# Two-stage delta-block kernel: row block substitution for the 128-row inverses, a float32 Gram row, and scratch-to-scratch copies of diagonal blocks

## What is computed

```python
k = k / jnp.linalg.norm(k, axis=-1, keepdims=True)
K = jnp.tril(jnp.einsum('ntc,nsc->nts', k, k), k=-1)
A = K + jnp.eye(T, dtype=x.dtype)
u = jax.scipy.linalg.solve_triangular(A, v, lower=True)
score = jnp.einsum('nsk,ntk->nst', q, k)
y = jnp.einsum('nst,ntv->nsv', score, lr * u)
return y @ out_w + out_b
```

```python
h = jax.nn.silu(gate) * up
return jnp.einsum('bsh,dh->bsd', h, wd)
```

## Time and profile before

| | before |
|---|---|
| median of 3 runs | 1599.51 us |
| the profiled execution's own time | 1598.77 us |
| span of its instructions | 1597.0 us |
| granted TensorE clock, share of full speed | 0.999 |
| TensorE matmul busy | 1576.0 us (99%) |
| TensorE weight load busy | 1409.5 us (88%) |
| DVE / ACT / POOL busy | 1140.3 / 778.4 / 780.5 us |
| keys stage, main stage | to about 266 us; from 268 us |

### The profile page before, as it was taken

How to read it: one execution, slowest core, us unless ns; L and a number is a source line. 1 busy time by engine, 2 the same in 40 slices (tenths; PEclk the granted TensorE clock), 3 DMA queues, 4 the chain that set the end, 5 groups by cost and what they waited for, 6 DMA issues and landing times.

```text
span 1597.0 us, 29857 instructions
## 1 busy us (share of the span) xinstructions
PE 1576.0 (99%) x10758; PEld 1409.5 (88%) x10758; DVE 1140.3 (71%) x2813; ACT 778.4 (49%) x1504; POOL 780.5 (49%) x918
## 2 busy tenths in 40 slices
PE   8999999899999999999999999999999999999998
PEld 8999998788888888888888888888888888888887
DVE  6767774577777677777776777877776666666664
ACT  5766664344444444444444444444444444444443
POOL 5446872344444554444445544444444444444442
PEclk9999999999999999999999999999999999999999
DMA  7989998112222322222222222222222222222200
GB/s 238 338 301 302 322 312 271 60 61 73 74 74 73 113 74 73 73 74 74 73 74 96 90 73 73 73 69 69 70 94 75 74 73 73 74 70 71 67 24 27
DMA packets 150164, 178.19 MB, mean 112 GB/s; under 512 B 78850, under 2 KB 132098, under 8 KB 141826
## 3 DMA queue, kind: packets, MB, share of 16 engines
q1 hardware_dynamic: 150018, 176.28, 33.4%
HBM read 98.64 MB, written 77.59 MB: 110 GB/s over the span
## 4 chain that ended last, share of the span: by engine, by line
PE 80%; DVE 2%; ACT 1%; POOL 0%; issue 0%; DVEq 0%; POOLq 0%; ACTq 0%
PE ps L174 33%; PE ps L1088 22%; PE ps L1098 11%; PE ps L1008 5%; PE ps L1019 4%; PE ps L1002 4%; PE ps L1129 0%; DVE z_lo L1452 0%; PE ps L246 0%; DVE low L198 0%; DVE low L218 0%; POOL work L1624 0%; DVE bs L1592 0%; ACT h_hi L1287 0%; DVE late L1477 0%
## 5 line engine op out<-in xcount | busy, mean ns | idle before, releaser
L1664 POOL TENSOR_TENSOR hl<-late,hh 128x512 fp32r<-128x512 f32 x128 | 165.3, 1291 | 207.2 <-ACT hh L1270 207.2
L1098 PE MATMUL ps<-wdT,hh 128*128 128x256 f32 x744 | 198.3, 303 | 0.0
L1265 ACT ACTIVATE late<-ps 128x512 f32<-128x512 f32 x192 | 114.3, 595 | 169.7 <-PE ps L1088 169.7
L1447 DVE TENSOR_TENSOR late<-ps,late 128x512 f32<-128x512 f32 x192 | 132.7, 691 | 87.5 <-PE ps L1088 85.9
L1274 ACT ACTIVATE z_hi<-ps 128x256 fp32r<-128x256 f32 x128 | 48.9, 382 | 288.4 <-PE ps L1019 288.4
L1098 PE MATMUL ps<-wdT,hl 128*128 128x256 f32 x744 | 181.8, 281 | 0.3 <-DVE hl L1452 0.3
L1270 ACT ACTIVATE hh<-late 128x512 fp32r<-128x512 f32 x192 | 120.8, 629 | 109.7 <-DVE late L1447 109.7
L1610 POOL TENSOR_TENSOR sc<-ls,mhalf 128x4 f32<-128x4 f32 x64 | 65.1, 1016 | 192.9 <-DVE ls L1414 192.9
L1646 POOL TENSOR_TENSOR xhm_lo<-xh,xhm_hi 128x1024 fp32r<-128x1024 f32 x32 | 76.4, 2386 | 163.3 <-DVE xhm_hi L1523 163.3
L1088 PE MATMUL ps<-xh3T_hi,wgT 128*128 128x512 f32 x384 | 153.4, 400 | 1.1 <-DVE xh3T_lo L1452 1.1
L1088 PE MATMUL ps<-xh3T_lo,wuT 128*128 128x512 f32 x384 | 152.1, 396 | 0.0
(11 more groups left out here) (212 smaller groups left out, 4690.7 us busy)
## 6 DMA issues: line engine op xcount, KB each, us to landing
xhT_scratch<-xhTk SPq DMA_DIRECT2D x32, 1024.0 KB, 6.8
xhT<-xhT_scratch SPq DMA_DIRECT2D x32, 1024.0 KB, 6.3
gg_scratch<-late SPq DMA_DIRECT2D x32, 640.0 KB, 4.2
gg<-gg_scratch SPq DMA_DIRECT2D x32, 640.0 KB, 3.9
xk<-in_L_attn_x_dram SPq DMA_DIRECT2D x32, 512.0 KB, 5.5
xt<-in_L_attn_x_dram SPq DMA_DIRECT2D x32, 512.0 KB, 4.0
out_dram<-late SPq DMA_DIRECT2D x31, 512.0 KB, 2.9
low_scratch<-late SPq DMA_DIRECT2D x128, 16.0 KB, 3.0
```

Source lines behind the costliest of these rows:

```text
L1098: mm = pe.matmul(ps[:, (FG, FU)[j // 2], (j % 2) * C:(j % 2 + 1) * C], part[:, h, blk(j)], wdT[:, h, :], start=(h == 0 and part is hh), st ...
L1265: act.activation(sg[:, h % 2, :], ps[:, FG, :], ACT.Silu, scale=QUANT).then_inc(sg_ev[h], 1)
L1447: dve.tensor_tensor(hf[:, h % 2, :], ps[:, up_bank(h), :], sg[:, h % 2, :], ALU.mult).then_inc(hf_ev[h], 1)
L1664: pool.tensor_tensor(hl[:, h, :], hf[:, h % 2, :], hh[:, h, :].bitcast(F32), ALU.subtract).then_inc(hl_ev[h], 1)
```

## The change

- **Levels.** One tensor xinv takes the place of x32 and x64. The three levels now make one row block of 32 each: rows 32 to 63 (32 columns), rows 64 to 95 (64 columns), rows 96 to 127 (96 columns). `below` copies PSUM into the part of xinv left of the diagonal; no addition, and the ACT copy of the last columns goes. Since xinv is used until the last `pe_zstep`, SP loads the next diagonal blocks after z_ps[0] and not after x128_ev.
- **Gram row 0.** The product of the first 128 tokens with themselves is made by two float32 matmuls from float32 copies (xhT0, pT0), not by six fp32r ones. ACT makes the copies: four 128x128 copies per sequence, each ahead of the signal to DVE.
- **Diagonal blocks.** For sequences 16 to 31 the four small stores of the keys stage go; `next_slot` copies their blocks from gg_scratch to low_scratch, 32 DMAs in a row for slot 2 and again for slot 3, then waits for them.
- **DVE order.** The inversion step at place 4 moves behind `dve_z(0)` and `dve_lo`; in the set-up `stats(dve, 2)` moves behind `dve_xhT(0)`.

```diff
@@ keys stage @@
-                for a in range(QPB):
+                for a in range(QPB if n < DIRECT else 0):
                     sp.dma_start(low_v[n][a], ggk[n % 2][a * SUB:(a + 1) * SUB, OFF:GW].rearrange("p (j c) -> p j c", c=P)
                                  [:, :, a * SUB:(a + 1) * SUB]).then_inc(low_out[n % 2], 16)
...
                 setup_lr(dve)
-                stats(dve, 2)
                 setup_s(dve)
                 dve_xhT(dve, 0)
+                stats(dve, 2)
...
                     act.wait_ge(xhT_ps[k], n + 1)
-                    act.activation(xhTk2[n % 3][0][:, k, :], ps[:, T0 + k, :], ACT.Copy).then_inc(xhT_hi[k], 1)
+                    act.activation(xhTk2[n % 3][0][:, k, :], ps[:, T0 + k, :], ACT.Copy)
+                    act.activation(xhT0[n % 3][:, k, :], ps[:, T0 + k, 0:P], ACT.Copy).then_inc(xhT_hi[k], 1)
...
-                row(0, 0, 0, 0, 2 + P)
+                for k in range(CB):
+                    pe.matmul(ps[:, G0, 0:2 + P], xhT0[n % 3][:, k, :], pT0[n % 2][:, k, :], start=(k == 0), stop=(k == CB - 1))
@@ main stage, PE @@
-                        pe.wait_ge(xd_tail, i + 1)
-                    pe.matmul(ps[:, A1, 0:C], x64[:, j, :], wt[:, j, :], start=True, stop=True).then_inc(z_ps[j], 1)
+                    pe.matmul(ps[:, A1, 0:C], xinv[:, j, :], wt[:, j, :], start=True, stop=True).then_inc(z_ps[j], 1)
...
-                        pe_level(pe, A1, p_of, x32, 0, REST, slice(0, P), xa_ps)
+                        pe_level(pe, A1, p_of, xinv, 0, SUB, slice(SUB, HALF), xa_ps)
...
-                        pe_level(pe, A0, p_of, x64, 0, HALF, slice(HALF, P), xb_ps)
+                        pe_level(pe, A0, p_of, xinv, 0, HALF, slice(HALF, REST), xb_ps)
...
-                        pe_level(pe, A1, p_of, x64, 0, SUB, slice(REST, P), x128_ps)
+                        pe_level(pe, A1, p_of, xinv, 0, REST, slice(REST, P), x128_ps)
@@ main stage, ACT and DVE @@
-                        act.activation(x64[:, :, REST:P], x32[:, :, REST:P], ACT.Copy).then_inc(xd_tail, 1)
...
-                def plus(dve, bank, w, rows, src_ps, done, i):
+                def below(dve, bank, w, rows, src_ps, done, i):
                     dve.wait_ge(src_ps, i + 1)
-                    dve.tensor_tensor(x64[rows, :, 0:w], levels(bank, w, rows), x32[rows, :, 0:w], ALU.add).then_inc(done, 1)
+                    dve.tensor_copy(xinv[rows, :, 0:w], levels(bank, w, rows)).then_inc(done, 1)
...
-                    dve_invert(dve, m, r, 4, 5)
                     if down:
                         dve_out(dve, i, 1)
                     if att:
                         dve_z(dve, i, 0)
                     if mlp:
                         dve_lo(dve, x3l, x3h, (FO0, FO1), x3h_ev, x3l_ev, i)
-                    dve_invert(dve, m, r, 5, 6)
+                    dve_invert(dve, m, r, 4, 6)
@@ main stage, SP @@
-                    sp.wait_ge(x128_ev, n)
-                    sp.wait_ge(xd_tail, n)
-                    load_inv(sp, n, x32, inv_v)
+                    sp.wait_ge(z_ps[0], n)
+                    load_inv(sp, n, xinv, inv_v)
...
+                def copy_low(sp, n):
+
+                    for a in range(QPB):
+                        blocks = bass.AP(tensor=gg_d.tensor, offset=gg_d[n].offset + OFF + a * (SUB * GW + SUB),
+                                         ap=[[GW, SUB], [P, TB], [1, SUB]])
+                        sp.dma_start(low_v[n][a], blocks).then_inc(low_copied, 16)
...
                         sp.wait_ge(inv_out, 32 * (m + 1))
-                        lows_stored(sp, GROUP * (m + 3))
+                        grams_stored(sp, GROUP * (m + 3))
+                        for q in range(GROUP * (m + 2), GROUP * (m + 3)):
+                            copy_low(sp, q)
+                        sp.wait_ge(low_copied, 16 * QPB * GROUP * (m + 1))
                         sp.dma_start(lanes[0][:, :], low_slot[m + 2]).then_inc(lanes[3], 16)
```

More of the change, by code:

```diff
@@ L79, in delta_block_kernel @@
     INV_STEPS = 2 + 2 * (SUB - 1)
+    DIRECT = 2 * GROUP
     with ExitStack() as ctx:
@@ L130, in delta_block_kernel @@
         gg = sb("gg", [P, GW])
-        x32 = sb("x32", [P, TB, P])
+        xinv = sb("xinv", [P, TB, P])
         xT32 = sb("xT32", [P, TB, P])
@@ L155, in lows_stored @@
             for q in range(2):
-                eng.wait_ge(low_out[q], 16 * QPB * ((n + 1 - q) // 2))
+                eng.wait_ge(low_out[q], 16 * QPB * ((min(n, DIRECT) + 1 - q) // 2))
         ready = ctx.enter_context(nc.semaphore("ready"))
@@ L272, in delta_block_kernel @@
             pT2 = [(t[:, 0, :, :], t[:, 1, :, :]) for t in pT]
+            pT0 = [sb(f"pT0{q}", [P, CB, 2 + P], c=pre) for q in range(2)]
             pads, loaded = sem("pads"), sem("loaded")
@@ L310, in setup_pool @@
                 pool.memset(one4[:, :], 1.0)
-                pool.memset(x32[:, :, :], 0.0).then_inc(x32_zero, 1)
+                pool.memset(xinv[:, :, :], 0.0).then_inc(x32_zero, 1)
                 pool.memset(xT32[:, :, :], 0.0).then_inc(x32_zero, 1)
@@ L342, in setup_lr @@
                 dve.wait_ge(wlr_done, CB)
+                for q in range(2):
+                    dve.tensor_copy(pT0[q][:, :, 0:2], wlr[:, :, :]).then_inc(lr0_done, 1)
                 for q in range(2):
@@ L406, in delta_block_kernel @@
             xhTk2 = [(t[:, 0, :, :], t[:, 1, :, :]) for t in xhTk]
+            xhT0 = [sb(f"xhT0{q}", [P, CB, P], c=pre) for q in range(3)]
+            lr0_done = sem("lr0_done")
             x_in, xhT_out = sems("x_in", 3), sems("xhT_out", 3)
@@ L494, in stored @@
                 wait(eng, gg_out[n % 2], 16 * (n // 2))
-                wait(eng, low_out[n % 2], 16 * QPB * (n // 2))
+                wait(eng, low_out[n % 2], 16 * QPB * (min(n, DIRECT + n % 2) // 2))
             def act_g(act, n):
@@ L545, in act_pT @@
                     act.wait_ge(pT_ps[k], n + 1)
-                    act.activation(pT2[n % 2][0][:, k, 2:2 + T], ps[:, P0 + k, :], ACT.Copy).then_inc(pT_hi[k], 1)
+                    act.activation(pT2[n % 2][0][:, k, 2:2 + T], ps[:, P0 + k, :], ACT.Copy)
+                    act.activation(pT0[n % 2][:, k, 2:2 + P], ps[:, P0 + k, 0:P], ACT.Copy).then_inc(pT_hi[k], 1)
             def make_xh(act, n):
@@ L656, in keys_pe @@
                         pe.wait_ge(lr_lo, 2)
+                        pe.wait_ge(lr0_done, 2)
                     if n >= 1:
@@ L760, in load_first @@
                 sp.wait_ge(x32_zero, 2)
-                for t, v in ((x32, inv_v), (xT32, invT_v)):
+                for t, v in ((xinv, inv_v), (xT32, invT_v)):
                     for a in range(QPB):
@@ L913, in delta_block_kernel @@
             p1 = mb("p1", [P, TB, P])
-            x64 = mb("x64", [P, TB, P])
             HALF = P // 2
@@ L940, in delta_block_kernel @@
             assert INV_EACH * (GROUP - 1) > INV_STEPS and SLOTS >= 3
+            low_copied = sem("low_copied")
             inv_in, gg_in, xhT_in, dg_in, xin, out_st = sem("inv_in"), sem("gg_in"), sem("xhT_in"), sem("dg_in"), sem("xin"), sem("out_st")
             rho_made = sems("rho_made", 3)
-            xd_tail, p1_zero, flipped = sem("xd_tail"), sem("p1_zero"), sem("flipped")
+            p1_zero, flipped = sem("p1_zero"), sem("flipped")
             pT_ps, pT_ev, xa_ps, xa_ev, xb_ps, xb_ev = (sem("pT_ps"), sem("pT_ev"), sem("x_a_ps"), sem("x_a_ev"),
@@ L1309, in act_body @@
                         act_hh(act, i - 1, HB - 1)
-                    if att:
-                        wait(act, inv_in, i * 32 * QPB)
-                        after(act, z_ps[0], i)
-                        act.activation(x64[:, :, REST:P], x32[:, :, REST:P], ACT.Copy).then_inc(xd_tail, 1)
                     if mlp:
@@ L1502, in dve_body @@
                         dve.tensor_copy(gl2[0][:, :], gg[:, 0:OFF]).then_inc(gl_hi, 1)
-                        plus(dve, A1, REST, slice(0, P), xa_ps, xa_ev, i)
+                        below(dve, A1, SUB, slice(SUB, HALF), xa_ps, xa_ev, i)
                     if mlp:
@@ L1508, in dve_body @@
                     if att:
-                        plus(dve, A0, HALF, slice(HALF, P), xb_ps, xb_ev, i)
+                        below(dve, A0, HALF, slice(HALF, REST), xb_ps, xb_ev, i)
                     dve_invert(dve, m, r, 0, 1)
                     if att:
-                        plus(dve, A1, SUB, slice(REST, P), x128_ps, x128_ev, i)
+                        below(dve, A1, REST, slice(REST, P), x128_ps, x128_ev, i)
                     if mlp:
```

## The result

The changed kernel takes 1604.68 us (median of 8 runs, 1603.54 to 1606.12), the one before 1599.76 us (median of 8, 1598.92 to 1600.44). The ratio is 1.0032, 95% interval 1.0022 to 1.0041: slower by 0.3%, 4.9 us, where 17.8 us less was forecast. The profiled execution took 1604.33 us.

The account below looks back on a forecast made before the run. The prediction took PE (TensorE) to set the pace nearly everywhere. Gram row 6.7, levels 9.9 and moved step 1.2 made 17.8 us off the profiled 1598.77: 1581.0, or 1581.7 us with 0.74 added for the median; range 1577 to 1590.

Parts of the forecast that it names:

- Gram row 0: Keys stage on PE: two records fewer per sequence, 0.21 us each sequence, 6.7 us over 32.
- ACT copies: Keys stage: four copies of 273 ns, at most 1.1 us per sequence on ACT, covered, cost nil.
- DMA binds: Rival, keys stage: DMA has no room, sequences 0 to 15 gain nothing, 3.4 us lost, 1585 us; chance 0.12.
- Levels: Main stage on PE: three levels fall from 1.77 to 1.41 us; 0.31 us per sequence taken, 9.9 us over 32.
- upper bound of this term: Levels: at most 0.41 us per sequence, 13 us in all, if both new forms ran at four fifths.
- Moved inversion step: Iterations 6, 14 and 22: 0.3 to 0.45 us of PE's wait comes back, 1.2 us over three.
- Later inverse loads: SP's loads of xinv after the last `pe_zstep`: 15 us of room, cost nil.
- VectorE's third level: Wide third-level copy on DVE ahead of `pe_zstep(3)`: under 1.09 us against 1.60 us of MLP matmuls, cost nil.
- set-up: Moved `stats(2)` lets DVE start the first low parts earlier, the ACT copies eat it: nil.
- Copies: SP's 32 copies at 0.45 us each, 14.4 us: DVE 0.5 us late, PE not delayed, nil; reserve some 2.5 us.
- the rival's own rule: PE waits at `pe_gate_up(4)` once a copy takes 0.53 us on SP; each further 0.1 us costs 3.2 us per slot.
- copies slower than stores: Rival on SP: dearer DRAM-to-DRAM copies make PE wait; gain gone at 0.81 us each, 1612 us at 1.0; chance 0.09.

Follow-up runs that it names:

- e1: The changed kernel without its copies, the diagonal blocks of all 32 sequences stored from SBUF in the keys stage as before: 1590.85 us.
- e7: The kernel before with the float32 first Gram row alone, its ACT copies and the later `stats(dve, 2)`; all stores kept: 1596.37 us.
- e9: The kernel before with the new levels and later inverse loads alone, without the moved inversion step: 1595.71 us.
- e3: The changed kernel with the diagonal-block load of sequences 8 and 16 issued ahead of the slot's copies, all 64 copies kept: 1588.05 us.
- e12: e3 with the first level made wide again, 128-column weights in place of 32: 1603.66 us.
- e4: The changed kernel with m_lo put ahead of `dve_up(2)` on VectorE in each iteration, copies and late load kept: 1597.44 us.
- e6: The changed kernel with 24 idle TensorE products in iterations 7 and 15 during the wait for m_lo: 1601.67 us.
- e10: The changed kernel with each slot's same bytes copied by 16 DMAs of 256 pieces instead of 32 of 128: 1587.81 us.
- e13: The changed kernel with its 64 copies spread over iterations 1 to 15, behind each one's last load, none in `next_slot`: 1588.78 us.

## Why the prediction was wrong

**Gram row 0: right in the changed kernel.** Forecast 0.21 us per sequence and 6.7 us; the period fell from 7.53 and 7.54 us in turn to 7.31 and 7.34 (the 7.46 that I had read was too short, the difference was right), and the keys stage ends 6.9 us sooner. By the 81 ns of the Trainium skill (TensorE: Matmul & The Clock Gate, Back-to-back issue gap) it would have been 5.2 us, an estimate; the rows of the trace were the better source. The ACT copies were covered, as said. The rival "DMA binds" is wrong: sequences 0 to 15, which keep their stores, gain the same 0.2 us each. But the row with all stores kept gives 5.8 us (e1) or 5.5 us (e7) at the end of the keys stage, by one wait in SP's queue of which the prediction had nothing, and alone it gave 4.2 us of the time.

**Levels: the mechanism right, the size less than half.** Forecast 0.31 us and 9.9 in all; the slots gave 1.94 - 1.76 = 0.18 us, the ordinary iteration 0.09 to 0.14, and the edit alone 4.1 us (e9). The new records ran as forecast (32, 56 and 82 ns, against 34, 57 and 85). The term that failed is 8 x (121 - 34) = 0.70 us for the first level, which measured 0.97 - 0.42 = 0.55. The 121 ns came from a mean over the group, and 8 x 121 ns is the whole slot, its change-over included: records were 112 ns apart. The 34 ns left the change-over out. And the new one is dear: the next group starts 181 ns after the last record of the narrow first level (175 in e3), against 112 ns behind the wide one. Behind the other two levels this distance is 149 and 176 ns, against 152 and 126 before. That the next group's weight load of 128 columns (188 ns in the traces) has no long matmul to hide behind is my reading, and no run tests it. Of the 0.18 us, some 0.06 are lost between the first level and the second, and 0.04 behind the third. What takes them stays open; e12 shows only that it isn't a bound of another engine. The upper bound of this term was also wrongly worked out: with both new forms at four fifths, 8 x (34 + 46 + 68) = 1.18 us, the gain would be 0.59 us and not 0.41.

**Moved inversion step: nearly right.** 1.2 us forecast, 0.8 us measured in iterations 6, 14 and 22.

**Later inverse loads, VectorE's third level, set-up: nil, right.** e1 and e3 hold all of these, and none of their iterations but iteration 1 is longer than before.

**Copies: wrong, and it decided the sign.** The step reads: "PE needs that result only at `pe_gate_up(4)`, behind 24 products of 256 columns ... Nil, but with only some 2.5 us in reserve." Three things in it failed.

1. The price on SP. I took 0.45 us from loads of xT from DRAM to SBUF; a copy from DRAM to DRAM took 0.644 us from start to start, and one 1.68. That is 32 x 0.19 = 6.2 and 1.1 us more. The last copy landed 1.5 us after the end of its issue, not 3.0, and GpSimd had dg in 2.2, not 2.8, which gives 2.1 back: `dve_up(2)` ran 5.1 us later than forecast. With the price alone, the rival's own rule (waiting from 0.53 us on, 3.2 us per 0.1) gives (0.644 - 0.53) x 32 = 3.6 us per slot. In e4 the wait that is left measured 4.0 and 3.3 us, though through ScalarE's silu, which the rule did not have. At 3.6 us the change would still have gained: 1581.7 + 7.3 = 1589 us by the prediction's own terms, and 1588.05 + 7.3 = 1595 from e3; e4, with the slower clock behind its wait, took 1597.44.
2. The reserve wasn't there. The 24 products are the y products, which wait for m_lo, and m_lo stands in VectorE's queue right behind `dve_up(2)`. I followed the late result to the engine that reads it, and not to what was queued behind the waiting instruction. In the kernel before, m_lo ended 0.4 us ahead of the first y product, and that was all the reserve. VectorE and TensorE in before:

```profile
576.22 0.68 DVE L1452 TENSOR_TENSOR m_lo<-m,m_hi 128x512 fp32r<-128x512 f32 x1
577.30 0.28 PE L174 MATMUL ps<-m_hi,xhT 128*128 128x256 f32 x1
```

   So the wait is 5.7 us and not 4.0.
3. The clock. TensorE standing for 5.7 us was followed by 4.6 us at half clock (1.2 GHz), 2.1 us lost (e6 gets 2.4 back in iteration 7). No bound of mine had such a term.

Sum per slot: 5.7 + 2.1 = 7.8 us; twice that is 15.6, and the trace shows 15.4. Against it stand 6.9 us of the keys stage and some 4 us of the other main iterations (0.1 us each, and 0.9 in 6, 14 and 22), and iteration 1 took 0.8 us more: together some 5 us, as measured. The rival "copies slower than stores" had the right place and SP's part of the mechanism, with chance 0.09; its argument against, that all small transfers issue at 0.45 us whichever way they go, rested on rows of which none had DRAM at both ends. The Trainium skill's rule on transfers under 512 bytes (DMA: Bandwidth & Descriptors, Specifications), cited there, pointed at the right part, but what cost the time was the issue on SP and not the transfer. The copies land in 2.1 us (median), the stores of the same pieces in 2.6. Since both have pieces of 128 bytes, no run shows what the rule itself is worth.

**The version that beats both.** e3 (1588.05 us), e10 (1587.81) and e13 (1588.78) keep the whole change and take away only what the copies held up: 0.7 to 0.8% faster than before. Their intervals overlap.

## What to carry to other kernels

When an edit adds work to a DMA queue, multiply the count of DMAs by an issue time taken from a DMA with the same endpoints and shape, and write down the deadline of each load behind it. Then follow the first late one not only to its reader but to everything queued behind that reader on its in-order engine: a wait of a small operation holds up results that have long been ready. Add the clock to the price of a stall of TensorE, and give each group of records its change-over on both sides of a difference.
